# Scores of a batch's first query tile by key, and the second query tile first, in a fused attention and FFN kernel

## The reference

```python
qkv = layernorm(x) @ w_qkv                  # 32 query heads, 8 key/value heads, D = 128
scores = einsum('bqhgd,bkhd->bhgqk', q, k) * D ** -0.5
bias = -slope[head] * sqrt(q_pos - k_pos)   # -inf above the diagonal
attn = softmax(scores + bias)
x = x + einsum('bhgqk,bkhd->bqhgd', attn, v).reshape(B, S, 4096) @ w_o
h = layernorm(x)
dots = softmax(h @ centroids.T / 0.1)       # 64 clusters
hits = dots > 0.01
dense = h @ weight.T + bias_ffn
out = x + where(any(hits, 1)[:, None] & any(hits, 0)[assignments], dense, 0)
```

## Time and profile before

| | us |
|---|---|
| median of 3 runs | 1258.83 (1258.37 to 1260.3) |
| span of the profiled execution | 1257.8 |
| TensorE busy | 1243.5, 99% |
| VectorE busy | 755.8, 60% |
| ScalarE busy | 757.0, 60% |
| GpSimd busy | 516.1, 41% |
| transfers issued by SyncE, share of the 16 DMA engines' span | 31.0% |

### The profile page before, as it was taken

The page is one execution under the profiler, slowest core; times in us unless marked ns, Lnnn a source line. Parts: engine busy times, 40 slices in busy tenths (PEclk is TensorE's granted clock), DMA queues, the critical chain, the costliest instruction groups (busy, mean ns, idle before and its releaser), DMA issues.

```text
span 1257.8 us, 21956 instructions
## 1 busy us (share of the span) xinstructions
PE 1243.5 (99%) x6200; PEld 1052.0 (84%) x6200; DVE 755.8 (60%) x2150; ACT 757.0 (60%) x2171; POOL 516.1 (41%) x476
## 2 busy tenths in 40 slices
PE   9899999999999999999999999999999999999998
PEld 7788888888888888888888888888888888888787
DVE  7777555555655555556555555655555565676677
ACT  5877556666665566666555566665566666655543
POOL 4521726227432546226442465327362264224223
PEclk9999999999999999999999999999999999999999
DMA  6522334334342334333333343324243343422103
GB/s 201 168 94 92 122 104 150 117 108 150 93 132 98 116 127 145 114 114 123 114 117 100 129 142 120 126 90 130 96 149 117 108 150 112 138 68 90 62 17 134
DMA packets 162522, 147.15 MB, mean 117 GB/s; under 512 B 10048, under 2 KB 123968, under 8 KB 162496
## 3 DMA queue, kind: packets, MB, share of 16 engines
q1 hardware_dynamic: 156672, 128.48, 31.0%
q0 software_dynamic: 5824, 18.36, 4.9%
HBM read 84.67 MB, written 62.13 MB: 117 GB/s over the span
## 4 chain that ended last, share of the span: by engine, by line
PE 90%; DVE 4%; ACT 4%; issue 1%; DMA 0%; POOL 0%; DVEq 0%; SPq 0%; ACTq 0%
PE ps L1319 84%; PE ps L1420 3%; PE ps L1421 1%; ACT prob L731 1%; ACT prob L722 1%; PE ps L1339 1%; DVE ring_whole L985 1%; DVE stats L898 0%; PE ps L1349 0%; DVE qT_lo L960 0%; DVE prob L1022 0%; DMA acc<-in_L_attn_hidden_states 0%; DVE rs L927 0%; PE ps L1451 0%; ACT ring_whole L685 0%
## 5 line engine op out<-in xcount | busy, mean ns | idle before, releaser
L1319 PE MATMUL ps<-xnT,wqkv_hi 128*128 (+2 forms) x1560 | 480.3, 389 | 0.0
L551 POOL TENSOR_TENSOR ring<-ring_whole,pT_hi 128x512 fp32r<-128x512 f32 x189 | 244.0, 1291 | 476.2 <-ACT pT_hi L711 475.8
L1319 PEld LDWEIGHTS ps<-xnT,wqkv_hi 128*128 128x128 f32 x1560 | 289.7, 188 | 59.5 <-issue 1.6
L722 ACT ACTIVATE prob<-prob,negmax 128x128 f32<-128x128 f32 (+1 forms) x512 | 226.8, 444 | 180.8 <-DVE negmax L1022 180.0
L1319 PE MATMUL ps<-xnT,wqkv_lo 128*128 (+1 forms) x780 | 302.7, 388 | 0.0
L731 ACT ACTIVATE prob<-prob,rinv 128x128 f32<-128x128 f32 (+1 forms) x512 | 190.3, 445 | 62.4 <-DVE rinv L1030 62.4
L1319 PE MATMUL ps<-wo_hi,oT_hi 128*128 128x512 f32 x512 | 201.8, 394 | 0.0
L1319 PE MATMUL ps<-wo_lo,oT_hi 128*128 128x512 f32 x512 | 199.8, 390 | 0.0
L1319 PE MATMUL ps<-wo_hi,oT_lo 128*128 128x512 f32 x512 | 199.4, 389 | 0.0
L1319 PEld LDWEIGHTS ps<-xnT,wqkv_lo 128*128 128x128 f32 x780 | 146.4, 188 | 30.3
L1002 DVE TENSOR_TENSOR acc<-ps,acc 128x512 f32 (+1 forms) x128 | 88.5, 691 | 127.4 <-PE ps L1319 127.4
(11 more groups left out here) (148 smaller groups left out, 1730.7 us busy)
## 6 DMA issues: line engine op xcount, KB each, us to landing
turned<-ring_whole SPq DMA_DIRECT2D x189, 256.0 KB, 2.1
ring_whole<-turned SPq DMA_DIRECT2D x189, 256.0 KB, 3.0
turned_v<-vT SPq DMA_DIRECT2D x32, 256.0 KB, 2.0
vT<-turned_v SPq DMA_DIRECT2D x31, 256.0 KB, 2.7
raw<-in_L_attn_w_qkv POOLq DMA_DIRECT2D x28, 256.0 KB, 3.1
raw<-in_L_attn_w_o POOLq DMA_DIRECT2D x28, 256.0 KB, 3.3
raw<-in_L_attn_w_qkv POOLq DMA_DIRECT2D x28, 128.0 KB, 3.2
acc<-in_L_attn_hidden_states SPq DMA_DIRECT2D x3, 1024.0 KB, 7.7
```

The source lines that it names most:

```text
L551: pool.tensor_tensor(ring_slot(c), whole_slot(c), pT_hi[:, c % 2, :].bitcast(F32), ALU.subtract).then_inc(pT_lo_done, 1)
L722: ins = act.activation(s, s, ACT.Exp, bias=negmax[:, n:n + 1], scale=-1.0, accum_out=rowsum[:, n:n + 1])
L1319: ins = pe.matmul(dst, l, r, start=start and m == 0, stop=stop and m == n - 1)
```

## The change

Scores of the first query tile are computed the other way round: k's high or low part is stationary and the first 128 queries of all four heads move, 512 columns. The three passes are three matmuls a batch (`scores_by_key`), and add up in one PSUM bank. The result stands as key x (head, query) and must be turned. VectorE transposes its 32x32 blocks out of PSUM (`turn_scores`) into a score tile, which is `prob`'s tile 0 for batch 0 and `vT` for batch 1; SyncE stores the tile to DRAM and loads it back (`scores_out`, `scores_in`); then VectorE's custom instruction adds the bias, with both inputs in SBUF. The adds of L1015 are gone. A unit has four transfers more, 18.

The second query tile of each batch now goes first, in scores, softmax, chunks and output tiles (`TILE_OF`), since the first one's scores come back later. The six bias steps of a unit are numbered e = 0 to 5, of which e = 2 and e = 5 are those of the turned blocks. Step 5, the exps 3 to 5 and the normalising of batch 1 are done in the body of the next unit. In the program for the tail the chunks are reordered alike.

The core of the diff (table numbers, the loop's other reorderings and the tail are left out):

```diff
+        def score_tile(b):
+            return vT[:] if b else prob[:, 0, :]
+        def head_slices(e):
+            b, part = e // 3, e % 3
+            if part < 2:
+                pair = part
+                return [(h, 4 * (2 * b) + h, prob[:, 1 + pair, (h % 2) * SEQ:(h % 2 + 1) * SEQ]) for h in (2 * pair, 2 * pair + 1)]
+            by_head = score_tile(b).rearrange("p (i h c) -> p h i c", i=P // BLK, h=HPG)
+            return [(h, 4 * (2 * b + 1) + h, by_head[:, h]) for h in range(HPG)]
...
+            return (b, 1, part) if part < 2 else (b, 0, 0)
+        def pair_of(c):
+            b, qt, _ = chunk_of(c)
+            return 2 * b + 1 - qt
+        TILE_OF = (1, 0, 3, 2)
         def ring_slot(c):
             return ring[:, c % RING, :]
-        LAST_CHUNK = (0, 2, 3, 5)
+        LAST_CHUNK = (1, 2, 4, 5)
...
+            def scores_out(v, b):
+                sp.wait_ge(keys_turned, v * 2 + b + 1)
+                sp.dma_start(turned_s[b], score_tile(b)).then_inc(s_out[b], 16)
+            def scores_in(v, b):
+                sp.wait_ge(s_out[b], v * 16 + 16)
+                sp.dma_start(score_tile(b).rearrange("p (i x) -> p i x", i=P // BLK),
+                             turned_s[b].rearrange("(i r) (j x) -> (r j) i x", i=P // BLK, j=P // BLK)).then_inc(s_in[b], 16)
+            def turn_first(v):
+                scores_out(v, 0)
+                scores_in(v, 0)
+                scores_out(v, 1)
+                turn_out(v, 0)
+                scores_in(v, 1)
+                turn_out(v, 1)
+                turn_in(v, 0)
+                turn_in(v, 1)
+                turn_out(v, 2)
+                turn_in(v, 2)
...
+            scores_out(0, 0)
             for h in range(2, HPG):
                 sp.wait_ge(raw_split, NC + h - 1)
                 load_o(0, h)
-            turn_half(0, 0)
-            turn_half(0, 1)
+            scores_in(0, 0)
+            turn_out(0, 0)
+            turn_out(0, 1)
+            turn_in(0, 0)
+            turn_in(0, 1)
+            scores_out(0, 1)
+            scores_in(0, 1)
+            turn_out(0, 2)
+            turn_in(0, 2)
+            turn_second(0)
...
+                    exps(u - 1, 3)
+                    exps(u - 1, 4)
                     pT_hi_part(u, 0)
-                    exps(u - 1, SCORE_BANKS - 2)
-                    exps(u - 1, SCORE_BANKS - 1)
...
-                    if attn and i < 2:
-                        normalise(u - 1, 2 + i)
                     if attn:
                         at = i - lag
-                        if at in (0, 2, 3):
-                            oT_hi_part(u, {0: 0, 2: 1, 3: 2}[at])
-                        if -1 <= at < CHUNKS - 2:
+                        if i == 0:
+                            normalise(u - 1, 2)
+                            pT_hi_part(u, 1)
+                        elif i == 1:
+                            exps(u - 1, 5)
+                        if at in (1, 2):
+                            oT_hi_part(u, at - 1)
+                        if 0 <= at < CHUNKS - 2:
                             pT_hi_part(u, at + 2)
+                        if i == 2:
+                            normalise(u - 1, 3)
...
+            def turn_scores(u, b):
+                dve.wait_ge(s_mm, u * BIASED + 3 * b + 1)
+                if b == 0:
+                    if not is_first(u):
+                        dve.wait_ge(p_turned, u * CHUNKS - 3)
+                else:
+                    dve.wait_ge(v_lo_done, u + 1)
+                dve.transpose(score_tile(b).rearrange("p (j h c) -> p h j c", h=HPG, c=BLK),
+                              ps[:, score_bank(u, 3 * b), :].rearrange("p (h r j) -> p h j r", h=HPG, j=P // BLK)).then_inc(keys_turned, 1)
...
-                if not (is_first(u) and i < 4):
-                    dve.wait_ge(p_turned, u * CHUNKS + {0: -2, 2: 0, 4: 1, 6: 3}[i // 2 * 2])
-                dve.wait_ge(s_mm, u * SCORE_BANKS + i + 1)
-                if qt == 0:
-                    h0, _, tile, col, _ = heads[0]
-                    dve.tensor_tensor(prob[:, tile, col:col + 2 * P].rearrange("p (h k) -> p h k", h=2),
-                                      ps[:, score_bank(u, i), :].rearrange("p (h s k) -> p h s k", h=2, s=2)[:, :, 1, :],
-                                      bias[:, h0:h0 + 2, P:SEQ], ALU.add).then_inc(lo_biased, 1)
-                    dve.wait_ge(lo_biased, u * 4 + 2 * b + i % 2 + 1)
+                if part == 2:
+                    dve.wait_ge(s_in[b], u * 16 + 16)
+                else:
+                    if b == 1:
+                        dve.wait_ge(p_turned, u * CHUNKS + 2)
+                    elif not is_first(u):
+                        dve.wait_ge(p_turned, u * CHUNKS - 1)
+                    dve.wait_ge(s_mm, u * BIASED + 3 * b + part + 2)
                 dve.sem_inc(dve_marks, 1)
-                for h, bank_col, tile, col, n in heads:
-                    s = prob[:, tile, col:col + (qt + 1) * P]
-                    ins = dve.tensor_tensor_reduce(
-                        out=s, in0=ps[:, score_bank(u, i), bank_col:bank_col + (qt + 1) * P], in1=bias[:, h, :] if qt else s,
-                        scale=-1.0, scalar=BIGGEST, op0=ALU.add, op1=ALU.min, accum_out=negmax[:, n:n + 1])
+                for h, n, s in head_slices(e):
+                    if part == 2:
+                        raw_scores, to_add = s, bias[:, h, P:SEQ].rearrange("p (i c) -> p i c", c=BLK)
+                    else:
+                        raw_scores, to_add = ps[:, score_bank(u, 3 * b + 1 + part), (h % 2) * SEQ:(h % 2 + 1) * SEQ], bias[:, h, :]
+                    ins = dve.tensor_tensor_reduce(out=s, in0=raw_scores, in1=to_add, scale=-1.0, scalar=BIGGEST, op0=ALU.add,
+                                                   op1=ALU.min, accum_out=negmax[:, n:n + 1])
                 ins.then_inc(scores_biased, 1)
...
+                        add_bias(u - 1, 5)
                         invert_sums(u - 1, 2)
                     if proj and i < PROJ_OUTS - 1 and not (i == 0 and is_second(u)):
                         proj_lo(u, i)
                     if proj and i == PROJ_OUTS - 1:
                         turn_v(u)
                     if attn:
-                        if i == 0:
+                        if i == 1:
+                            turn(u - 1, 3)
+                            turn(u - 1, 4)
                             invert_sums(u - 1, 3)
-                            turn(u - 1, 3)
-                        if i - lag in (0, 2, 3):
-                            oT_lo_part(u, {0: 0, 2: 1, 3: 2}[i - lag])
-                        if i == 1:
-                            turn(u - 1, 4)
                         if i == 2:
                             turn(u - 1, 5)
+                        if i - lag in (1, 2):
+                            oT_lo_part(u, i - lag - 1)
...
+                if is_first(u):
+                    turn_scores(u, 0)
                     add_bias(u, 0)
                     add_bias(u, 1)
-                if attn:
-                    oT_lo_part(u, 3)
-                if attn:
-                    add_out(u, 1)
+                    invert_sums(u, 0)
+                    add_bias(u, 2)
+                    turn(u, 0)
+                    turn(u, 1)
+                    turn_scores(u, 1)
+                    proj_lo(u + 1, 0)
+                    add_bias(u, 3)
+                    add_bias(u, 4)
+                    invert_sums(u, 1)
+                    turn(u, 2)
+                    return
...
+            def scores_by_key(u, b):
+                bank_free(u, 3 * b)
+                at = slice(b * SEQ, b * SEQ + P)
+                dst = ps[:, score_bank(u, 3 * b), :].rearrange("p (h q) -> p h q", h=HPG)
+                three_pass(dst, [((kT[:, 2 * b, 0, :], kT[:, 2 * b, 1, :]), (qT_hi[:, :, at], qT_lo[:, :, at]))],
+                           True, True).then_inc(s_mm, 1)
```

More of the change, by code:

```diff
@@ L812, in body @@
                     cluster_exps(p)
[L813 to L821 removed]
+                exps(u, 0)
+                exps(u, 1)
+                if is_first(u):
+                    v_hi_part(u)
+                normalise(u, 0)
+                if is_first(u):
+                    proj_hi(u + 1, 0)
+                exps(u, 2)
+                normalise(u, 1)
             def first_w_hi(c):
```

296 lines of the change are left out of this document (135 added, 161 removed).

## The result

| | before | after |
|---|---|---|
| median of the runs, us | 1259.2 (4 runs) | 1288.06 (4 runs) |
| ratio, 95% interval | | 1.0231 (1.0217 to 1.0246) |
| span of the profiled execution, us | 1257.8 | 1285.9 |
| TensorE busy, us | 1243.5 | 1241.3 |
| TensorE idle, us | 14.3 | 44.6 |

The change makes the kernel 29 us slower. The forecast was 1253.0, faster.

A forecast was written before the change was run, and what follows sets the result against it. TensorE, busy 99% of the span, was taken as the bound. -16.2 (blocks) + 7.1 (start) + 0.5 (w_o units) + 0.5 + 0.4 - 0.3 + 2.2 (tail) = -5.8 us, so 1253.0; own range 1248 to 1257, full range 1244.5 to 1259.5.

The forecast's parts named there:

- The block on TensorE: Scores blocks, two a unit: 0.680 us each instead of 0.933, gaining 0.507 a unit, 16.2 over 32 units.
- The rule weighed there: Skill's matmul timing rule: old block 660 ns, new 647, so 0.8 us gained in all; kept as a rival.
- The lock: VectorE operations with two SBUF inputs stand behind GpSimd: at most a few tenths a unit, 0 to 3 us in all.
- a slack of 2.3: Loop: VectorE turns the second key block till 32.45; TensorE wants that bank at 34.80.
- GpSimd's pT_lo: Loop: the first chunk's low part is done at 42.3 and wanted at 43.68, slack 1.3 us.
- the tail's 2.2: Unit 31 and behind the loop: waits on VectorE and ScalarE cost 1.4 to 3.5 us, taken as 2.2.
- Rival (d): Port lock at its worst in the loop costs 3 to 5 us: 1257, no change; chance 0.08.
- The start: Units 0 and 1: TensorE waits on the second score tile's chain; costs 7.1 us against the ideal, 5.3 to 9.
- w_o units: The 7 units that split w_o: slack for the second chunk only 0.1 to 0.3, so 0.5 us put.
- Units 30, 31 and tail: End of the program: unit 30 waits 0.4 us, unit 31's layer norm gains 0.3, the tail costs 2.2.
- Rival (c): Loop: vT score tile's round trip beyond 9.0 us delays 28 units; at 9.3, 10 us more, 1263; chance 0.07.

The follow-up runs named there:

- experiment 1: Changed kernel with the bias of the turned blocks left out, VectorE taking a minimum of the score tile alone: 1263.58 us, ratio 1.0041.
- experiment 7: Changed kernel with GpSimd waiting for the first turned block's bias before v's low part in units that split QKV weights: 1265.75 us, ratio 1.0050.
- experiment 4: Changed kernel with the two w_o loads issued in the next unit, behind the low parts of chunks 0 to 2: 1283.22 us, ratio 1.0189.
- experiment 5: Changed kernel with TensorE kept busy by identity transposes during its two waits in unit 1: 1289.53 us, ratio 1.0239.
- experiment 2: Changed kernel with only a quarter of each score tile stored and loaded back, same waits: 1259.63 us, ratio 1.0000.

## Why the prediction was wrong

*The block on TensorE*: right. 0.68 each, 35.56 against 36.08 for an undisturbed unit. The rule weighed there came out as the trace had said: by the Trainium skill, "TensorE: Matmul & The Clock Gate", section "Wait - 56ns, not 53.3ns?", the unit would by an estimate have gained 0.8 / 32 = 0.03; it gained 0.52.

*The lock*: the step that failed. It said that two blocked operations would be 2.6 us against a slack of 2.3, "at most a few tenths a unit", and 0 to 3 us in all. Measured: one operation stood 2.4 us too long, close to the size that I had put, and the seven units lost 23.7, shown by experiments 1 and 7. The size of the delay was right; what it cost was not, for three reasons, each with its number. First, I held it against the wrong slack, that of the second key block's bank. The chain that decided runs over the reciprocal, normalise and the chunks to GpSimd's pT_lo, and I had myself written 1.3 for it. Second, I walked that chain with median landings. A delay of 1.9 at the turn became 4.0 at the landing (experiment 7), since it moved the first chunk's load behind the w_o loads; without those w_o loads the excess was 15.8 (experiment 4). Third, in three of the seven units the wait was followed by some 3.7 us at the 1.2 GHz level, another 1.7 each, which stood in no sum of mine.

Had these been put in, with the doubling as unit 8 shows it, the sum would have read 7 x (2.4 + 2.1 - 1.3) + 3 x 1.7 = 27.5 us, and 7 x (2.4 - 1.3) = 8 with the first reason alone. -5.8 with either added is on the other side of zero. In the sum as it stood the lock was no term of its own, only a part of the tail's 2.2, though the text gives it 0 to 3 in the loop; and the own range, 1248 to 1257, is not what its bounds add up to: 1250.4 to 1258.2. Rival (d) named the mechanism and priced it at 3 to 5.

*The start*: right in kind, too small. Predicted 6.1 slower up to unit 2 (7.1 less the gain of two units), measured 9.6. The chain was the one described, link by link, but its terms were not. The two chunks' stores ahead took 3.4 and 3.3 instead of 2.1, so the second tile's store was issued at 47.15 and not at 44.7, and took 4.75 instead of 2.1. Its load, which I had given 5.2, took 3.0, and it landed at 54.9 instead of 52.0. That 52.0 was no further off is in part luck, two errors against one. The fifth projection started at 59.75, 3.25 later than the 56.5 that I had put, and that is nearly all of the 3.5 by which the start was mis-sized. The granted clock was 0.54 from 52.7 to 65.4, which was in no sum; experiment 5 does not show that it counted.

*w_o units*: 0.5 in all was forecast over the gain of 0.5 each; they lost 3.6 more than that. The lock is at most a part of it: with GpSimd's wait (experiment 7) they still last 2.8 us longer than six undisturbed ones, against 4.2. I did not follow the rest. *Unit 29* was not in the sum: 3.1 us, most of it waits of 1.07 and 1.70 for VectorE at 1116.89 and 1121.32. With quarter tiles (experiment 2) the first is gone and the second is 1.2. *Units 30, 31 and tail*: predicted 1.3, measured 1.5. Rival (c), a late second score tile in the loop, did not occur: its load landed in 3.3 and VectorE waited for it once in the whole run, in the start.

What stays open: why a chunk's store takes 3.2 to 4.5 when other transfers are under way, since no experiment took the stores apart; why the clock fell behind three of the seven waits and not behind the longest; and how much of experiment 2's gain is the shorter load's timing and how much the free DMA engines.

## What to carry to other kernels

An operation of VectorE that gets a second input in SBUF has a new partner to wait for: look at what GpSimd does at that moment, for how long without a pause, and follow the delay to the end of the chain, through the transfers as they land in that place and not at their median. If TensorE would wait some 2 us for it, the time at a lower clock behind can come on top: here it did in three of seven waits of 1.4 to 2.9 us, so it is a term with a range and not a fixed one. Where the order of two engines decides over tens of microseconds by a few tenths, write the order down with a semaphore.

## What the runs showed of the hardware

- A VectorE operation with both inputs in SBUF, started 0.48 us before a GpSimd operation in the records, still stood behind it and a second one that followed without a gap: 2.73 us, released when GpSimd paused 0.09 us. Before units 8 to 28 of the changed kernel and of experiment 5 all those that started 0.44 to 0.61 us ahead stood, and the one 0.62 ahead (experiment 5) and those further ahead did not. The changed kernel before unit 4 is an exception: one that started 0.68 ahead stood 2.16 us, through the first GpSimd operation alone, and the next stood 0.90 behind the second. The Trainium skill, "SBUF - State Buffer", section "SBUF: two separate sides", says that the one that starts first gets the ports for the whole instruction; by these records that was VectorE, whose 0.29 us would even have ended before GpSimd's start, so the start in the record is not the moment that decides, or the rule is not so simple. The measurement decides for planning: 0.6 us ahead was not enough, unless GpSimd was held by a semaphore (experiment 7, 0.46 to 0.55 ahead, none stood).
- Operations of VectorE that read PSUM, the transposes and the minimum with one input in SBUF did not stand in the same stretches: in the changed kernel the addition and the transpose from PSUM at 305.86 and 306.55 took 0.68 each beside GpSimd's wqkv_lo, and the minimum took 0.28 in the bias operation's place (experiment 1).
- GpSimd's issue of a DMA (302.95 to 303.66) did not hold VectorE's third operation, 302.99 to 303.28, nor did the one of 302.20 to 302.92 the two of experiment 7.
- Behind 2.0 us without work (unit 8) TensorE first ran at full clock for 1.15 us, and then 3.7 us at a granted clock of 0.54. Behind 1.90 us (unit 4) and 2.86 us (unit 16) the clock of the unit stayed at 1.00.
